# First attention stage: reciprocals left in PSUM, zz products and small maxima reordered, two slots exchanged

## The reference

```
q, k, v = x Wq^T + bq, x Wk^T + bk, x Wv^T + bv      # 16 heads of 64
scores  = q k^T / 8, causal (-inf above the diagonal)
att     = softmax(scores) / 8
x       = x + (att v as 1024 columns) @ proj
```

## Time and profile before

| what | before |
|---|---|
| median of 3 runs | 1251.79 us (1251.09 to 1256.2) |
| the profiled execution | 1252.09 us, span 1250.3 us |
| busy in the span | TensorE 1057.7 us (85%), VectorE 789.5 (63%), ScalarE 706.4 (56%), GpSimd 565.5 (45%) |
| first attention, units 0 to 15 | from about 41 us to 685 us |
| mean granted TensorE clock | 0.909 of full |

### The profile page before, as it was taken

The page is one execution under the profiler, slowest core; times in us unless marked ns, Lnnn a source line. Parts: engine busy times, 40 slices in busy tenths (PEclk is TensorE's granted clock), DMA queues, the critical chain, the costliest instruction groups (busy, mean ns, idle before and its releaser), DMA issues.

```text
span 1250.3 us, 18772 instructions
## 1 busy us (share of the span) xinstructions
PE 1057.7 (85%) x6927; PEld 635.1 (51%) x6927; DVE 789.5 (63%) x1454; ACT 706.4 (56%) x1031; POOL 565.5 (45%) x482
## 2 busy tenths in 40 slices
PE   4878779787978788877976669999999939999998
PEld 3545445554655545544553632223322228878876
DVE  6766675767676776667655542223422158999998
ACT  3444444444544454444542248999999937665664
POOL 2355555556565665555665000000000015878876
PEclk9788898888888998889988669999999968999999
DMA  2000000000000000002000000000000000311210
GB/s 82 7 7 8 1 7 7 7 1 7 7 8 7 2 8 7 7 1 50 1 1 1 1 2 7 12 12 12 11 12 9 9 5 2 119 69 67 84 50 34
DMA packets 24928, 23.52 MB, mean 19 GB/s; under 512 B 17613, under 2 KB 20317, under 8 KB 23821
## 3 DMA queue, kind: packets, MB, share of 16 engines
q1 hardware_dynamic: 24844, 22.42, 6.3%
HBM read 19.20 MB, written 1.11 MB: 16 GB/s over the span
## 4 chain that ended last, share of the span: by engine, by line
PE 51%; DVE 30%; issue 10%; ACT 5%; SPq 1%; POOL 1%; DMA 1%; DVEq 0%; ACTq 0%; POOLq 0%
DVE zz L697 10%; PE banks L1054 9%; PE banks L469 7%; PE banks L1042 6%; DVE big L1359 5%; PE banks L443 3%; PE banks L396 3%; PE banks L339 3%; PE banks L488 3%; PE banks L477 2%; PE banks L449 2%; DVE banks L676 2%; PE banks L445 2%; PE banks L447 2%; DVE mxa L671 2%
## 5 line engine op out<-in xcount | busy, mean ns | idle before, releaser
L773 POOL TENSOR_TENSOR pacc<-pacc,prob 128x1024 f32<-128x1024 f32 (+3 forms) x160 | 280.3, 1752 | 123.7 <-ACT prob L569 114.0
L569 ACT ACTIVATE prob<-banks 128x1024 f32<-128x1024 f32 (+1 forms) x160 | 148.4, 939 | 216.0 <-PE banks L449 203.9
L1063 ACT ACTIVATE prob<-banks 128x1024 f32<-128x1024 f32 x256 | 238.7, 1099 | 21.4 <-PE banks L1042 21.4
L1392 POOL TENSOR_TENSOR big<-prob,big 128x512 fp32r<-128x512 f32 x108 | 165.0, 1547 | 59.7 <-ACT big L1342 33.2
L469 PE MATMUL banks<-prob,v 128*64 128x512 f32 (+3 forms) x768 | 146.9, 513 | 2.1 <-POOL prob L762 2.1
L443 PE MATMUL banks<-big 64*128 64x512 f32 (+3 forms) x384 | 81.2, 418 | 69.6 <-DVE mxa L671 69.6
L697 DVE TENSOR_TENSOR zz<-zr,yneg 64x256 f32<-64x256 f32 x128 | 138.5, 1082 | 1.4
L1054 PE MATMUL banks<-prob,v 128*32 128x512 f32 x1024 | 137.1, 608 | 0.8 <-DVE pacc L1071 0.3
L1348 ACT ACTIVATE prob<-banks,w 128x512 f32<-128x512 f32 x144 | 94.4, 685 | 71.5 <-PE banks L1310 71.3
L1008 POOL TENSOR_TENSOR wqkv<-wqkv 64x512 f32<-64x512 f32 x8 | 8.3, 1032 | 261.7 <-DVE wqkv L1004 261.7
L762 POOL TENSOR_SCALAR_AFFINE_SELECT prob<-prob 128x256 f32<-128x256 f32 x128 | 51.1, 411 | 147.1 <-ACT prob L569 147.1
(11 more groups left out here) (221 smaller groups left out, 1757.9 us busy)
## 6 DMA issues: line engine op xcount, KB each, us to landing
prob<-gate_rows SPq DMA_DIRECT2D x8, 1024.0 KB, 4.5
w<-in_experts SPq DMA_DIRECT2D x9, 514.0 KB, 3.6
wqkv<-in_wqkv SPq DMA_DIRECT2D x16, 193.0 KB, 2.4
x<-in_x SPq DMA_DIRECT2D x4, 256.0 KB, 4.1
zz<-pacc SPq DMA_DIRECT2D x64, 16.0 KB
wpr<-pacc SPq DMA_DIRECT2D x64, 16.0 KB
out<-x SPq DMA_DIRECT2D x4, 256.0 KB, 2.3
wpr<-in_wpr SPq DMA_DIRECT2D x1, 512.0 KB, 5.9
```

What stands on the lines that cost most here:

```text
L569: act.activation(pr[:, g % NRING, :, 0:wd], banks[:, 2 * (j % 2):2 * (j % 2) + 2, 0:wd], ACT.Exp, scale=SCALE0).then_inc(s_exp, 1)
L773: pool.tensor_tensor(pacc[:, half, :, o:BLK], pacc[:, half, :, o:BLK], p_[:, :, at:at + wd], ALU.add).then_inc(s_padd, 1)
L1063: act.activation(prob[:, n % NP1, :], banks[:, 2 * (n % 3):2 * (n % 3) + 2, :].rearrange("p b c -> p (b c)"), ACT.Exp, scale=2 * SCALE1).t ...
L1392: pool.tensor_tensor(act2[1][:, tb % 2, i, :], hid[:, tb % 2, i, :], act2[0][:, tb % 2, i, :], ALU.subtract).then_inc(s_hlP, 1)
```

## The change

Five edits, all in the first attention.

1. **The reciprocal stays in PSUM.** The second Newton operation writes to bank 4 or 5, in place; `yneg` is gone, and the four products read one operand from SBUF and one from PSUM. As the bank is now read by the products, `pv_pe` waits for them (`s_zz`) where it waited for the Newton step (`s_nw`).
2. **Products moved in VectorE's order.** Those of the second half of unit u - 1 stand at the end of step 1, right behind their Newton step (before: in step 2, between runs 4 and 5). Those of the first half of unit u stand in step 4 between runs 8 and 9 (before: at the end of step 4, behind the two remainders). In step 2 VectorE takes run 5 before run 4, and TensorE's scores of slot 6 wait for one of the two only. In step 3 the Newton step of the first half comes before the addition to x.
3. **Small maxima first.** Run 0 (512 columns in two pieces) and run 1 (256 columns) change places.
4. **v in step 3.** On TensorE the first v projection goes from the end of step 2 to step 3 behind the sums, and the projection `out_pe` comes behind it; the second v projection goes between the products of slots 4 and 5. In step 4 the q and k projections and their rounding come before the transpose and the rows of maxima.
5. **Slots 8 and 9 exchanged:** slot 8 is now the one of 256 columns, slot 9 the one of 384 + 128.

```diff
-        yneg = sb("yneg", [P, BLK])
...
-                 (1, ((4, 0, 0, 512),)), (1, ((5, 0, 128, 384), (7, 384, 384, 128))), (1, ((6, 0, 256, 256),)))
+                 (1, ((4, 0, 0, 512),)), (1, ((6, 0, 256, 256),)), (1, ((5, 0, 128, 384), (7, 384, 384, 128))))
...
-        MAX_RUNS = [((0, 0, 0), (2, 0, P)), ((1, 0, 0),), ((3, 0, 0),), ((4, 0, 0),), ((5, 0, 0),), ((6, 0, 0),), ((7, 0, 0),),
+        MAX_RUNS = [((1, 0, 0),), ((0, 0, 0), (2, 0, P)), ((3, 0, 0),), ((4, 0, 0),), ((5, 0, 0),), ((6, 0, 0),), ((7, 0, 0),),
...
-                pe.wait_ge(s_mx, NR * (u + 1) + j)
+                pe.wait_ge(s_mx, NR * (u + 1) + (5 if j == 6 else j))
...
             elif j == 3 and not first:
-                pe.wait_ge(s_nw, 2 * u)
+                pe.wait_ge(s_zz, 2 * u)
...
+                elif i == 3:
+                    sums_pe(pe, u, 0)
                     if not last:
                         v_pe(pe, n, x_, bn, 0, 6)
-                elif i == 3:
                     if not first:
                         out_pe(pe, u - 1)
-                    sums_pe(pe, u, 0)
                     pv_pe(pe, u, w, 4, first)
-                    pv_pe(pe, u, w, 5, first)
                     if not last:
                         v_pe(pe, n, x_, bn, 1, 6)
+                    pv_pe(pe, u, w, 5, first)
                 else:
-                    if not last:
-                        turn_pe(pe, n, 0, 2)
                     if n < 2 * PAIRS - 1:
                         qk_pe(pe, n + 1, w, (n + 1) // PAIRS, 0)
                         qk_pe(pe, n + 1, w, (n + 1) // PAIRS, 1)
+                    if not last:
+                        turn_pe(pe, n, 0, 2)
...
-            dve.scalar_tensor_tensor(out=yneg[:, :], in0=banks[:, 4 + sbk, :], scalar=2.0, in1=y0[sbk][:, :],
+            dve.scalar_tensor_tensor(out=banks[:, 4 + sbk, :], in0=banks[:, 4 + sbk, :], scalar=2.0, in1=y0[sbk][:, :],
...
-                                            zr[sbk][HP[h], odd:BLK:2], yneg[HP[h], odd:BLK:2], ALU.mult)
+                                            zr[sbk][HP[h], odd:BLK:2], banks[HP[h], 4 + sbk, odd:BLK:2], ALU.mult)
...
-                    max_dve(dve, n, 2 * i)
-                if i == 2 and not first:
-                    z_dve(dve, u - 1, 1)
+                    max_dve(dve, n, 2 * i if i != 2 else 5)
+                if i == 4:
+                    z_dve(dve, u, 0)
                 if not last:
-                    max_dve(dve, n, 2 * i + 1)
+                    max_dve(dve, n, 2 * i + 1 if i != 2 else 4)
...
                         newton_dve(dve, u - 1, 1)
+                        z_dve(dve, u - 1, 1)
...
                 elif i == 3:
+                    newton_dve(dve, u, 0)
                     if not first:
                         xacc_dve(dve, u - 1)
-                    newton_dve(dve, u, 0)
                 elif i == 4:
                     if n < 2 * PAIRS - 1:
                         lo_dve(dve, n + 1, w, 0)
                         lo_dve(dve, n + 1, w, 1)
-                    z_dve(dve, u, 0)
```

More of the change, by code:

```diff
@@ L295, in build_kernel @@
                  (1, ((0, 0, 0, 512),)), (1, ((1, 0, 0, 512),)), (1, ((2, 0, 0, 512),)), (1, ((3, 0, 0, 512),)),
-                 (1, ((4, 0, 0, 512),)), (1, ((5, 0, 128, 384), (7, 384, 384, 128))), (1, ((6, 0, 256, 256),)))
+                 (1, ((4, 0, 0, 512),)), (1, ((6, 0, 256, 256),)), (1, ((5, 0, 128, 384), (7, 384, 384, 128))))
         NS = len(SLOTS)
         WIDTH = tuple(sum(piece[3] for piece in pieces) for _, pieces in SLOTS)
-        ADDED = (1, 3, 4, 5, 6, 7, 8, 9, 11, 12)
-        MASKED = {0: 1, 1: 3, 2: 4, 7: 5, 8: 7, 9: 8}
+        ADDED = (1, 3, 4, 5, 6, 7, 8, 9, 10, 12)
+        MASKED = {0: 1, 1: 3, 2: 4, 7: 5, 8: 6, 9: 8}
         NM = 8
-        MAX_RUNS = [((0, 0, 0), (2, 0, P)), ((1, 0, 0),), ((3, 0, 0),), ((4, 0, 0),), ((5, 0, 0),), ((6, 0, 0),), ((7, 0, 0),),
+        MAX_RUNS = [((1, 0, 0),), ((0, 0, 0), (2, 0, P)), ((3, 0, 0),), ((4, 0, 0),), ((5, 0, 0),), ((6, 0, 0),), ((7, 0, 0),),
                     ((4, 1, 0), (6, 1, P)), ((5, 1, 0),), ((7, 1, 0),)]
@@ L385, in max_pe @@
             elif r == 6:
-                pe.wait_ge(s_v, 2 * n + 1)
+                pe.wait_ge(s_mx, NR * n + 6)
                 if n == 1:
@@ L414, in v_pe @@
                     pe.wait_ge(s_v, 1)
+            elif k == 0:
+                pe.wait_ge(s_mx, NR * n + 7)
             else:
-                pe.wait_ge(s_mx, NR * n + (5, 7)[k])
+                pe.wait_ge(s_v, 2 * n + 1)
             for t in range(4):
@@ L463, in pv_pe @@
                 else:
-                    pe.wait_ge(s_nw, 2 * u - 1)
+                    pe.wait_ge(s_zz, 2 * u - 1)
             elif j == 3 and not first:
-                pe.wait_ge(s_nw, 2 * u)
+                pe.wait_ge(s_zz, 2 * u)
             for t, at, o, wd in pieces:
@@ L469, in pv_pe @@
                     mm = pe.matmul(banks[HP[h], 4 + half, o:BLK], v[:, w, t, HP[h]], pr[:, g % NRING, h, at:at + wd],
-                                   start=(t == 0), stop=(t == 4 * half + 2))
+                                   start=(t == 0), stop=(t == (2, 7)[half]))
             mm.then_inc(s_pv, 1)
@@ L636, in unit0_act @@
                     z_act(act, u, 0)
-                    if not last:
-                        v_act(act, n, x_, 0, 6)
                 elif i == 3:
@@ L641, in unit0_act @@
                     if not last:
+                        v_act(act, n, x_, 0, 6)
                         v_act(act, n, x_, 1, 6)
                 else:
-                    if not last:
-                        mrow_act(act, n, x_, 0, 2)
                     if n < 2 * PAIRS - 1:
@@ L648, in unit0_act @@
                         hi_act(act, n + 1, w, 1)
+                    if not last:
+                        mrow_act(act, n, x_, 0, 2)
         def lo_dve(dve, n, w, i):
@@ L797, in router_const_pe @@
                 pe.wait_ge(s_fca, 1)
-                pe.wait_ge(s_mx, NR + 5)
+                pe.wait_ge(s_mx, NR + 6)
                 pe.matmul(banks[:, 7, BLK // 2:BLK // 2 + NE0], wpT[:, :], simk[:, :], start=True, stop=True).then_inc(s_fcp, 1)
```

## The result

The changed kernel takes 1102.9 us (median of 4 runs, 1099.2 to 1104.4), the kernel before 1254.0 beside it (1251.1 to 1258.1): a ratio of 0.879, with a 95% interval of 0.875 to 0.883. That is faster, as forecast, but by 151 us and not by 131, and outside the range of 1108 to 1153.

A forecast was written before the change was run, and what follows sets the result against it. TensorE, with a 5 us wait set by VectorE's products stretched beside GpSimd, was taken as the bound. Savings of 122.5 us in units 1 to 13 and 8.2 in unit 14 took 1252.1 to 1121 us, range 1108 to 1153.

The forecast's parts named there:

- What bounds the kernel: TensorE sets the stage, with a 5 us wait set by VectorE's products, stretched by two SBUF operands beside GpSimd.
- Step 1: zz products with the reciprocal in PSUM: 0.445 us each, four in 1.78, VectorE spending 3.6 us a unit, not 9.05.
- Steps 2 and 3: TensorE's waits: 5.05 us before slot 6 falls to about 0.1; 1.38 at the q projection and 0.56 at run 9 go.
- Step 4: TensorE's clock stays full without long idles: 2.2 us at slots 6 and 7 plus 0.4 at the projection, 2.6 a unit.
- Step 5: End of a unit: TensorE done at 30.8 us, waiting 0.3 at slot 0 for VectorE's 5.66 us tail; unit 31.1.
- The sum: Whole kernel: 122.5 us from units 1 to 13, 8.2 from unit 14, nothing from units 0 and 15; 1121 us.
- The low end, 1108: Lower end of the time range, from units of 30.2 us: products at 0.41 us and VectorE's tail covered.
- B: A chain through VectorE stays before slot 6: unit 34.5 us, 1169 us in all, from 1141 to 1180; chance 0.14.
- C: Lock holds with a PSUM operand too, products stay at 6.34 and 2.71 us: unit 38.6, about 1227; chance 0.06.
- D: Slower: strided PSUM reads are slow or products blocked one by one, TensorE's queue behind them; 1281 us; chance 0.06.

The follow-up runs named there:

- e1: Kernel before with only the reciprocal kept in PSUM, every order, run and slot as before; 1140.9 us, ratio 0.910, units of 32.77 us.
- e3: Kernel before with GpSimd adding only one column of each tile, softmax sums left incomplete; 1129.5 us in one run, units of 32.69 us.
- e7: Changed kernel with products back at their old places in VectorE's order, reciprocals still in PSUM; 1127.8 us in one run, units of 31.47 us.
- run 0: Not a follow-up run: a unit's maximum run on TensorE, reduced by VectorE, 256 columns in the changed kernel; begins 1.03 us behind slot 0.
- e4: Changed kernel with one remainder written a second time, 0.70 us more VectorE work per unit; 1104.4 us in one run, units of 30.28 us.
- run 8: Not a follow-up run: a unit's maximum run on TensorE, reduced by VectorE in 0.95 us, ahead of products and run 9 in the changed kernel.
- e12: Changed kernel itself, run again unaltered; 1103.7 us over six runs, ratio 0.879 to the kernel before.
- e2: Changed kernel with the reciprocal back in SBUF, all orders and slots as changed; 1134.9 us, ratio 0.902, slowest and profiled run 1162.8 us.
- e9: Changed kernel with zz products cut to 8 of 256 columns from unit 1 on; 1101.2 us in one run, units of 30.10 us.
- e11: Changed kernel with the product with v of slot 1 moved from step 1 to step 2; 1103.7 us over six runs, ratio 0.880.

## Why the prediction was right or wrong

- **What bounds the kernel**: right. The products, stretched by GpSimd's additions, set the wait before slot 6; e1 and e3 show it from both sides. The page "SBUF — State Buffer" of the Trainium skill, section "SBUF: two separate sides", gives the shared lock to VectorE operations with two SBUF inputs or in a two-port mode; the 128 products at 402 to 425 ns, with one SBUF input, agree.
- **Step 1**: right in kind, too dear by 0.02. The line through 292 and 692 ns gave 425, the median is 419 and four take 1.71 us, not 1.78. The slower PSUM source of "VectorE: DVE Perf Modes" in the Trainium skill, section "The TRN2 errata", some 65 ns as an estimate from its cycles, does not show: 402 and 419 ns (least and median) with an operand in PSUM, 405 and 422 with both in SBUF and no long additions (e3). Nor does a step of two show a cost in either, as the line through two instructions without one gives 425.
- **Steps 2 and 3**: right. Slot 6 begins 15.1 us after the unit's start, forecast 15.0. The three waits are gone, and the new wait of the slot 3 product costs nothing where the products now stand (slots 2 and 3 are one row of 1.51 us at 301.29); where they don't, it costs 1.0 (e1, e7).
- **Step 4**: right in kind, with the granted clock at 1.00 from 78.5 to 530 us; the terms are off both ways. Slots 6 and 7 with their runs go from 302.73 to the sums' start at 305.63, 2.9 us where 4.67 stood in the earlier trace rows: 1.8 less and not 2.2. The projection takes 2.12 where it took 2.72: 0.6 less and not 0.4. TensorE's whole busy time in unit 8 fell from 32.85 to 30.06, 2.8 for the 2.6 that I took.
- **Step 5 failed**, in two terms. The larger: TensorE's own time, "done at 30.8", was 30.1, and that is 0.7 of the 1.0 us. The 0.4 of small waits that I added did not occur (all idle time of unit 8 is 0.07), the busy time fell by 0.2 more than the 2.6 of step 4, and the idle time before was 7.1 (39.98 less 32.85) where I had counted 7.0. With unit 8 at 40.0 these make 30.1.
- The smaller term, 0.3 us, is a wrong path: "5.66 together, before the next unit's slot 0". The two remainders of step 4 belong to the unit after next; slot 0 has long had its own, and only run 0 needs them. The timeline shows it: they began at 316.96 and took 1.40, to 318.36; slot 0 began at 317.78, run 0 at 318.81. e4 measured the slack. I had read the number in `scores_pe`, 4u + 2, as those of step 4, without counting. With the right count the forecast would have been 30.8, still 0.7 too long. VectorE's own times were near: it began run 8 at 25.3 after the unit's start (forecast 25.5) and ended the remainders at 30.7 (31.1). The 34.3 of run 8 had unit 7 begin 39.98 before unit 8, while it began 41.11 before it, at 328.25; the figure is right all the same for unit 8 itself (403.70 - 369.36).
- **The sum**, from one profiled execution to the other (22 us missed; 18 by the median of 1102.9): 1.0 us a unit too much makes 12.8. Unit 0, which I set at nothing, makes 2.6, and as e12 has 38.34 us there against 38.44, this part is likely the change's (the kernel before was profiled once); unit 15 makes 1.3. 5.6 are in the start and in the later stages, which no edit touches, so nothing shows them to be the change's; the start alone moves by 4.6 from run to run (e12). Unit 14 came out at 8.2, as forecast, but by luck: I had it end with VectorE's run 9 at 29.7, while TensorE was the bound there too, with a wait that I had not foreseen. As unit 14 has no q and k projections, its transpose comes early and waits 1.01 us for the exponential of slot 9, and slot 0 of unit 15 (498.10) follows the products with v without a gap. The low end, 1108, rested on a unit of 30.2, which was nearly met; it set units 0 and 15, the start and the later stages at nothing, and those put the time below it.
- **The rivals**: B, C and D did not occur. Both C and D were weighed low because of L655's 740 to 753 ns, and rightly. The price of C was wrong, though: e2 is all but its case (the changed order, with products that still stretch), and had 34.1 us a unit in its slowest run where I had worked out 38.6, by taking the 6.34 us of four products along to a place where they take 3.92.

## What to carry to other kernels

An instruction whose duration spreads sixfold for one shape is the place to start; look at what the other engines do beside it, and whether an operand can live elsewhere or the instruction can stand elsewhere, as either alone may bring most of the gain (here 111 and 117 of some 150 us). Where a wait is on a count, count it through to the unit that it belongs to before putting it on a path. When the engine that sets the pace has no idle left in its timeline, moving further work around it brings nothing (e9, e11), and a sum of single undos says little about a set of edits that rest on each other.

## What the runs showed of the hardware

- A VectorE product of two SBUF operands takes up to 2.65 us beside GpSimd's additions, and 0.42 in the median when these are short (e3, longest 0.87); with one operand in PSUM all 128 take 0.40 to 0.43 (402 to 425 ns, in e1 402 to 430), at a step of two in both.
- The clock can fall after a shorter idle than the 5 us of the kernel before. That kernel itself shows it: in unit 7 TensorE waited 1.54 us at the q projection, and the granted clock was low behind it; in unit 8, from which the prediction was worked out, the wait there was 1.38 and the clock held. Unit 7 took 41.11 us, unit 8 39.98. Of the waits there in units 1 to 14, 1.37 to 1.55 us long, nine were followed by a low clock and five were not, two of 1.54 us among these.

```profile
332.59 0.54 PE L339 MATMUL banks<-xhi,whl 128*128 128x512 f32 x1 [1.54 <-DVE mx L676]
...
332.59:336.80 4.21, 4.21 (x17) 2.57 (x19) 2.21 (x6) 2.19 (x6) 2.86 (x3) 0.59 0.00 0
373.53:377.70 4.17, 4.17 (x31) 2.81 (x33) 2.16 (x7) 3.05 (x8) 3.04 (x4) 1.00 0.00 0
```

- In e2, TensorE waited 2.04 us before slot 6, and within 2 us of its end the granted clock was low for a few us:

```profile
316.00:351.00 35.00, 32.09 (x263) 19.43 (x262) 27.24 (x58) 20.45 (x35) 25.86 (x24) 1.00 0.03 7
366.80:368.88 2.08, 0.04 (x2) 0.00 (x1) 2.05 (x3) 0.00 (x0) 2.00 (x4) 1.00 0.00 0
370.70:373.90 3.20, 3.20 (x18) 2.01 (x16) 2.04 (x6) 1.58 (x2) 2.71 (x3) 0.59 0.01 3
```

In the unit before (from 318.58 us) a wait of 2.05 us had left it at full, and that unit took 33.05 us where those with the low stretch took 34.3. So the same idle may or may not be followed by a low clock; no run here shows what decides it. The clock explains 1.25 us a unit; e2's runs spread over 43 us, 3 a unit, with a mean granted clock of 0.937 in the slowest and 0.952 to 0.960 in the others. Only the slowest was profiled, so whether the products meet fewer additions in the others stays open. Kernels without such an idle (e11, e12) spread over 3 and 7 us in six runs.
